# Two groups of queries and the first keys of two cross-attention stages made at the end of the stage ahead, and four stages' transfers reordered

## What is computed

```python
x = x + tanh(g_xattn[0]) * attention0(ln(x), ctx, ctx)      # 16 heads of 16
x = x + tanh(g_ffn[0])   * position_experts(ln(x))          # 8 experts, each for its 14 positions
x = x + tanh(g_xattn[1]) * attention1(ln(x), ctx, ctx)
x = x + tanh(g_ffn[1])   * lora_experts(ln(x))
x = x + tanh(g_xattn[2]) * decoder_block(ln(x), ctx)        # self-attention, cross-attention, relu layer
x = x + tanh(g_ffn[2])   * product_key_experts(ln(x))
x = x + tanh(g_xattn[3]) * attention3(ln(x), ctx, ctx, mask, padding)
x = x + tanh(g_ffn[3])   * routed_experts(ln(x))

def attention(query, key, value):
    q, k, v = heads(query @ Wq + bq), heads(key @ Wk + bk), heads(value @ Wv + bv)
    return merge(softmax(q @ k.T * scale) @ v) @ Wo + bo
```

## Time and profile before

| | us |
|---|---|
| median of 3 runs | 2893.66 (2892.99 to 2894.96) |
| the profiled execution's own time | 2895.43 |
| its span in the trace | 2893.7 |
| busy: PE, PEld | 2554.0 (88%), 2092.4 (72%) |
| busy: DVE, ACT, POOL | 1782.6 (62%), 1345.4 (46%), 1124.6 (39%) |
| the 16 DMA engines, mean share over the span | 42% |
| first cross stage begins, second, third, fourth | 313.85, 673.12, 1415.44, 2163.92 |

### The profile page before, as it was taken

One profiled execution on the slowest core, in us unless ns is written; L12 is line 12 of the kernel. 1 busy time (PEld: TensorE's weight loads), 2 busy tenths in 40 slices (PEclk: granted clock), 3 DMA queues, 4 the chain that ended last, 5 costly groups with the idle time before them and its releaser, 6 DMA issues.

```text
span 2893.7 us, 57252 instructions
## 1 busy us (share of the span) xinstructions
PE 2554.0 (88%) x21445; PEld 2092.4 (72%) x21445; DVE 1782.6 (62%) x3888; ACT 1345.4 (46%) x2700; POOL 1124.6 (39%) x1424
## 2 busy tenths in 40 slices
PE   7999789997997999869799898888868995999995
PEld 7999578794786777636477566667645884999995
DVE  5666578116784434268577445787777884566664
ACT  4444466324564121147456533444443663555563
POOL 3444411004113333247622233633543113677772
PEclk9999899997998999989789999889988996999997
DMA  8888865236660000053376300000008653565663
GB/s 229 239 244 241 220 180 166 100 120 157 164 192 16 1 1 1 19 149 87 83 190 166 125 17 6 0 1 1 1 18 212 170 136 132 195 216 205 205 222 111
DMA packets 145580, 357.06 MB, mean 123 GB/s; under 512 B 26064, under 2 KB 102480, under 8 KB 130816
## 3 DMA queue, kind: packets, MB, share of 16 engines
q1 hardware_dynamic: 133584, 268.38, 32.9%
q0 software_dynamic: 11760, 85.51, 8.3%
HBM read 260.55 MB, written 84.54 MB: 119 GB/s over the span
## 4 chain that ended last, share of the span: by engine, by line
PE 59%; DVE 11%; DMA 9%; POOL 6%; issue 6%; ACT 5%; SPq 2%; PEld 0%; POOLq 0%; PEldq 0%; ACTq 0%; DVEq 0%
PE ps L3156 8%; PE ps L1190 6%; PE ps L1200 6%; PE ps L1174 5%; DMA key_parts<-arena 5%; PE ps L3167 5%; PE ps L1745 3%; POOL arena L428 2%; PE ps L2347 2%; PE ps L2106 2%; PE ps L928 2%; PE ps L2340 2%; PE ps L2096 2%; PE ps L2056 2%; PE ps L1187 2%
## 5 line engine op out<-in xcount | busy, mean ns | idle before, releaser
L1304 ACT ACTIVATE arena<-ps 125x448 f32<-125x448 f32 x768 | 405.4, 545 | 293.0 <-PE ps L1190 289.3
L1337 DVE TENSOR_REDUCE arena<-ps 112x2 f32<-112x750 f32 x384 | 348.3, 930 | 97.8 <-PE ps L1174 96.3
L502 POOL TENSOR_SCALAR ln_var<-ln_mv 112x1 f32<-112x1 f32 x160 | 43.3, 270 | 746.7 <-DVE ln_mv L496 742.2
L1190 PEld LDWEIGHTS ps<-arena,wreg 98*125 98x125 bf16 x2304 | 217.7, 144 | 86.1 <-issue 45.3
L1190 PE MATMUL ps<-arena,wreg 98*125 98x112 bf16 x2304 | 238.8, 229 | 27.0 <-issue 17.5
L3156 PE MATMUL ps<-moe_x_r,moe_w_r 128*128 128x256 f32 x2016 | 254.4, 287 | 4.1 <-DVE arena L3312 2.7
L3156 PEld LDWEIGHTS ps<-moe_x_r,moe_w_r 128*128 128x128 f32 x2016 | 248.4, 194 | 7.3 <-DVE arena L3312 3.9
L1174 PE MATMUL ps<-wreg,arena 96*112 96x375 bf16 x768 | 203.6, 352 | 23.7 <-DMA arena<-arena 12.9
L1200 PE MATMUL ps<-arena 125*17 125x112 f32 x6144 | 201.8, 265 | 0.6 <-ACT arena L1304 0.6
L428 POOL TENSOR_TENSOR arena<-arena 128x375 bf16<-128x375 f32 x128 | 113.8, 913 | 171.2 <-ACT arena L365 171.2
L285 PE MATMUL ps<-kv_ctx_r,kv_w_r 128*128 128x376 f32 x768 | 145.9, 339 | 22.9 <-DVE kv_w_r L391 14.6
(11 more groups left out here) (367 smaller groups left out, 5860.8 us busy)
## 6 DMA issues: line engine op xcount, KB each, us to landing
wreg<-key_parts SPq DMA_DIRECT2D x288, 187.5 KB, 3.9
key_parts<-arena SPq DMA_DIRECT2D x128, 281.2 KB, 4.1
values<-arena SPq DMA_DIRECT2D x64, 357.0 KB
arena<-values SPq DMA_DIRECT2D x64, 357.0 KB
arena<-query_parts SPq DMA_DIRECT2D x84, 224.0 KB, 4.3
arena<-key_parts SPq DMA_DIRECT2D x96, 187.5 KB, 3.9
wreg<-in_e_w SPq DMA_DIRECT2D x16, 704.0 KB, 5.4
query_parts<-arena SPq DMA_DIRECT2D x14, 672.0 KB, 6.1
```

Of the source, the lines that this page charges most:

```text
L1190: mm = pe.matmul(ps[0:KN, bank, g * T:(g + 1) * T], keys[r][:, hd, c * KN:(c + 1) * KN], queries(b)[:, hd, :], start=not masked, stop=not ...
L1304: act.activation(probs[k % PROBS], ps[0:KN, 4 + k % 2, 0:GT], ACT.Exp, scale=scale).then_inc(at_probs, 1)
L1337: dve.tensor_reduce(negmax[r % 2][:, 2 * p:2 * p + 2], ps[0:T, 2 * (p % 2):2 * (p % 2) + 2, 0:S2], AX.X, ALU.max, negate=True).then_inc(at ...
```

## The change

`context_stage` and `position_experts_stage` get an object `CrossAhead` of the cross stage that follows. At their end they load keys 0 of that stage, project, split and (group 0) spread its groups 0 and 1. The cross stage then projects only groups 2 and 3: group 2 between the pairs of batch 0, group 3 behind `maxima(0, 0)` and one pair of batch 1. All four cross stages get another order on SP: values 2 and the store of group 3 move from step 0 to steps 1 and 2, and values 3 behind rows(2). In `self_stage` the gains are loaded ahead of group 1, and POOL's wait for them moves from the stage's start to its fourth batch. The diff without its places in memory:

```diff
@@ context_stage
                 step(B - 1, 1, None)
+                ahead.load_keys(sp)
@@ tensor
-                pe.wait_ge(kv_vout, B * NKV * 2)
-                for b in range(B - LAG, B):
-                    norm.turn(pe, b, turned(TURN_BANK + 2 * (b % 2)), LAG)
+                pe.wait_ge(loaded, ahead.q.ready)
+                pe.wait_ge(part_res, ahead.q.q0 - 2)
+                for g in range(AHEAD):
+                    ahead.q.project(pe, range(g, g + 1))
+                    if g == 0:
+                        pe.wait_ge(kv_vout, B * NKV * 2)
+                    norm.turn(pe, B - LAG + g, turned(TURN_BANK + 2 * g), LAG)
@@ scalar
+                ahead.q.high_and_middle(act, range(1))
                 norm.apply(act, B - 1)
+                ahead.spread(act, range(2))
+                ahead.q.high_and_middle(act, range(1, AHEAD))
+                ahead.spread(act, range(2, PARTS))
@@ vector
-                for b in range(B - LAG, B):
-                    evacuate(dve, b, turned(TURN_BANK + 2 * (b % 2)))
+                for g in range(AHEAD):
+                    ahead.q.remainders(dve, range(g, g + 1))
+                    evacuate(dve, B - LAG + g, turned(TURN_BANK + 2 * g))
@@ gpsimd
+                pool.wait_ge(ln_ready, norm.before("ready", B))
+                ahead.q.low(pool, range(AHEAD))
@@ cross_stage, sync
-                load_keys(sp, keys[0], kv, 0, 0)
+                if not ahead:
+                    load_keys(sp, keys[0], kv, 0, 0)
...
-                q.spread_first(sp, 0, group_q[0], Q_PART, group_in[0])
+                if not ahead:
+                    q.spread_first(sp, 0, group_q[0], Q_PART, group_in[0])
...
-                for g in range(1, G - 1):
+                for g in range(1, made_ahead or G - 1):
                     q.store(sp, g)
                 load_values(0, 0)
...
                 rows(0)
+                for g in range(made_ahead or G - 1, G - 1):
+                    q.store(sp, g)
...
                     if b == 0:
                         q.stored(sp, G - 2)
                         load_queries(1, range(len(Q_PART)))
+                    if b == 1:
                         load_values(2, 2)
+                        load_values(3, 3)
+                    if b == 2:
                         q.store(sp, G - 1, q_last)
-                    if has(b, 3):
+                    if b > 0 and has(b, 3):
                         at_least(sp, at_pv, (n0 + b) * STEPS if has(b, -1) else 0)
                         load_values(b + 3, place(3))
@@ tensor
-                q.project(pe, range(G - 1))
+                beside = made_ahead or G - 1
+                q.project(pe, range(made_ahead, beside))
...
-                        q.project_tile(pe, G - 1, tile, (chunk,))
-                arrived(1, 1, turn0)
-                pair(1, 1, 0)
-                maxima(0, 0)
-                pair(1, 1, 1)
+                        q.project_tile(pe, beside, tile, (chunk,))
+                if ahead:
+                    maxima(0, 0)
+                    arrived(1, 1, turn0)
+                    pair(1, 1, 0)
+                    q.project(pe, range(beside + 1, G))
+                    pair(1, 1, 1)
...
@@ vector
+                if ahead:
+                    q.remainders(dve, range(made_ahead, G - 1))
+                    reduce_pair(1, 1, 0)
                 q.remainders(dve, range(G - 1, G))
@@ self_stage
             def sync(sp):
+                norm.load(sp)
                 inputs.load(sp, 1)
-                norm.load(sp)
...
-                pool.wait_ge(loaded, loaded_all)
...
+                            if k == 3 and g * GB + b == 3:
+                                pool.wait_ge(loaded, loaded_all)
@@ position_experts_stage, sync
                 sp.wait_ge(loaded, following.ready)
+                sp.wait_ge(ffn_out, E * DC)
+                ahead.load_keys(sp)
+                ahead.spread(sp)
@@ tensor
                     if b % GB == GB - 1 and b > GB:
                         for q in range(GB):
                             norm.turn(pe, b - 2 * GB + 1 + q, slots[q % 2], 2)
+                        g = b // GB - 2
+                        if g >= 0:
+                            if g == 0:
+                                pe.wait_ge(loaded, following.ready)
+                            ahead.q.project(pe, range(g, g + 1))
@@ scalar
                         norm.evacuate(act, b - 1, slots[(b - 1) % 2])
+                    if b % GB == GB - 1 and b > GB and b < B - 1:
+                        g = b // GB - 1
+                        ahead.q.high_and_middle(act, range(g, g + 1))
@@ gpsimd
+                    if g >= G - AHEAD:
+                        pool.wait_ge(ln_ready, norm.before("ready", (g + 1) * GB))
+                        ahead.q.low(pool, range(g - G + AHEAD, g - G + AHEAD + 1))
+                        pool.wait_ge(part_lo, ahead.q.q0 + (g - G + AHEAD + 1) * DC)
@@ vector
+                    if g >= G - AHEAD:
+                        ahead.q.remainders(dve, range(g - G + AHEAD, g - G + AHEAD + 1))
```

More of the change, by code:

```diff
@@ L688, in load, with spread_first @@
                     self.weights.load(sp)
-            def spread_first(self, sp, kind, dest, order, arrived):
-                for level, made in enumerate((part_hi, part_mid, part_lo)):
+            def spread_first(self, sp, kind, dest, order, arrived, levels=range(PARTS)):
+                for level in levels:
+                    made = (part_hi, part_mid, part_lo)[level]
                     sp.wait_ge(made, self.q0 + (kind + 1) * DC)
@@ L728, in remainder, with high_and_middle @@
             def remainder(self, n):
-                return self.rest[n % len(self.rest)]
-            def high_and_middle(self, act):
+                return self.rest_ahead[n] if n < len(self.rest_ahead) else self.rest[n % len(self.rest)]
+            def high_and_middle(self, act, some=range(G)):
                 def middle(g, j):
```

108 lines of the change are left out of this document (73 added, 35 removed).

## The result

The changed kernel takes 2860.02 us (median of 4 runs, 2856.35 to 2865.80), the kernel before 2894.31 (2892.99 to 2895.72) beside it: a ratio of 0.9883, 95% interval 0.9863 to 0.9904, faster by 34.3 us. Forecast were 2859.5 and 34.3 us, with a range of 2848 to 2875. But the profiled execution of the changed kernel is its slowest, 2865.80 (span 2864.1) against 2895.43 before, so between the two traces only 29.6 us are to be found, and the runs of the changed kernel spread over 9.4 us where those of before spread over 2.7.

The account below looks back on a forecast made before the run. Bound by the way to PE's steady cross-stage steps: late queries, holes before step 2, POOL's late self-attention start. 23.3 + 0 + 0 + 11.0 = 34.3 us off 2895.43 gives 2861.1, median 1.8 lower: 2859.5; range 2848 to 2875.

Parts of the forecast that it names:

- 15.8: Starts of first and second cross stages: us from first pair to first scores, as PE waits for group 3.
- The order on SP: All four cross stages: rows(2) no longer last, holes and slow clock go; 5.3 + 8.5 + 6.0 + 3.5 = 23.3 us.
- The holes: PE idle before step 2 of the cross stages; given back 4.0 of 4.52, 4.4 of 5.79, 4.35 and 2.06 us.
- The clock's share: Slow clock behind the holes: 4.1 us in the second cross stage, 1.3, 1.7 and 1.4 in the others by hole length.
- The tail of the context stage: End of context stage: barrier 7.3 us later, first scores 1.0 earlier, nothing gained; between 6 lost and 6 gained.
- The tail of the experts' stage: End of position experts' stage: barrier at 683.0, first scores at 699.1 instead of 698.62, no gain; between 7 lost and 7 gained.
- The self-attention: Self-attention's start: POOL starts at 1267.4 instead of 1278.80; 11.0 us gained, between 8 and 11.4.
- The rival that spoke of the hole moving: Cross stages: values 2 or rows(3) become late instead; all 23.3 lost gives 2882.5, half 2871; chance 0.15.
- Tails in series: Ends of context and experts' stages: little overlaps, barriers about 11 us later than worked out, 2881; chance 0.08.
- Slower by the clock: First two cross stages: PE stays at clock 0.50 through steps, 2903 with four slow steps in each; chance 0.02.
- The clock rule: Starts of first two cross stages: pairs begin cold, each start some 2 us longer, 4 us less in the sum.
- other rule, of two rings on one set of engines: Context stage's end: sixth spreading transfer shares with keys 1, lands perhaps 1 us later; 33 instead of 34 in sum.

Follow-up runs that it names:

- SP's order alone: Kernel before with values 2 and 3 behind rows(2) and group 3's store in step 2, all cross stages: 2899.09 us, ratio 0.9945.
- context's tail: Changed kernel with next group's queries ahead of their step's values, position experts' stage and second cross stage's start as before: 2870.04 us, ratio 0.9861.
- spread by SP: Changed kernel with next group's queries ahead of their step's values and the context stage's spread issued by SP, not ACT: 2854.68 us, ratio 0.9845.

## Why the prediction was right, point by point

The total is right by luck in part: the order gave less than its 23.3 us, the experts' tail and the self-attention more than theirs, and the waits for queries took some back. Two small slips in its sums change nothing: 2861.1 less 1.8 is 2859.3, and 10.4 and 5.2 are 15.6, not 15.8.

**The order on SP, 23.3 us.** By the changed kernel's trace the four starts gave 1.8, 9.5 (to step 3), 5.9 and 5.7, 22.9 us, which looks like the forecast. It holds the experts' tail and the chance of two executions. Over the fourteen traces the four cross stages are shorter with the new order, waits for queries taken off (in the fourth not), by:

| cross stage | length taken | old order (3 traces) | new order | gain | forecast |
|---|---|---|---|---|---|
| first | C1 | 221.3 | 215.6 (3, no tail) | 5.8 | 5.3 |
| second | C2 | 358.8 | 354.0 (4, no experts' tail) | 4.8 | 8.5 |
| third | last spreading transfer to last marker | 205.7 | 203.0 (11) | 2.7 | 6.0 |
| fourth | last marker of the third to its own | 771.6 | 768.0 (11) | 3.6 | 3.5 |

The sum is 17 us, and SP's order alone measured 16 (10 to 22). Single traces of a row differ by 1 to 5.5 us. The holes went as told: no "issue" piece over 1.5 us before step 2 in any stage. The terms of the second and the third stage were too large. They rest on one trace of the kernel before, whose holes there are 5.79 and 4.35 us, while the two other kernels with the old order have 4.83 and 4.69, 3.27 and 3.87; and with the new order PE still stands 0.4 to 2.1 us wherever the chain waits for values 2 before step 2. The clock's share was not worked out by the rule given for it, either: by the lengths of the holes the 4.1 us would give 3.2, 3.1 and 1.5 for the other stages, not 1.3, 1.7 and 1.4. In the first two stages the changed kernel's own rows hide a swap, too. "Values 2 land about a microsecond after step 1 ends; in the second likewise" was too small for the order alone: without the tail steps 1 to 2 of the second stage are 13.8 to 15.5 us, 3 to 5 above a steady step. It became true by the experts' tail, which the forecast had priced at nothing.

**The tail of the context stage, 0.** Right: C1 is 215.4 us in the mean with it and 215.6 without. Its terms were less so: the barrier fell 8.6 us later, not 7.3, since ACT's issue was 0.96 us a transfer, not 0.61, within the 0 to 1.2 kept open. The last spreading transfer was taken at "some 4 us" and needs 5.26; the same transfer takes 5.36 in the kernel before. The first pair came 2.8 us earlier by the same clock of the start, not 4.2; the first scores (341.02, with the head start of 1.2) 1.1 us later, not 1.0 earlier. The profiled run lost 3.5 us to the forecast for this stage: its marker of step 2 stands 70.8 us behind the last remainder, those of the seven other traces with this tail 67.5 to 69.6, and of the three with SP's order and no tail 67.8 to 69.8. In nine of these eleven traces the chain waits for values 2 just before step 2; in the changed kernel's and in "context's tail" it does not, since step 1 itself comes late there, behind keys 2.

**The tail of the experts' stage, 0.** This is the step that failed. "The transfers have landed by then, so the first pair is at 683.3 instead of 687.38, and with the same 15.8 us the first scores at 699.1: no gain": on the scale of the kernel before (4.0 us added) the barrier fell at about 681, the first pair at 681.3 and the first scores at 698.9. That looks right, but only beside a trace whose own first scores are the earliest of seven; by the table above the first scores came 3 us earlier, and step 2 another 4. The prediction said that SP's work there lies beside an idle queue and did not ask what that work, out of the way, does for the next late transfer. The tail was worth some 6 us, near the end of the 7 kept open.

**The self-attention, 11.0.** 12.8 over the fourteen traces, 13.0 in the changed kernel's, 11.6 (7.3 to 16) alone. POOL's start moved by 11.3, as told; in the cross stages the prediction had counted the slow clock behind a stall and here left it out.

**The changes of groups: no term.** The forecast took the steady steps as untouched because nothing in the diff touches them. Their length is, but one step in four waits for a load, and that wait was longer in this trace: the second stage lost 3.6 us behind its step 3 and the third 2.3 behind its step 2, nearly all of it at changes of groups. The steady steps are as before (10.74). By Q the loss is 5.6 us in the pair of traces and 4.7 in the means (13.0 against 8.3), which just about cancels the experts' tail.

**The rival that spoke of the hole moving** (0.15) was half right in mechanism for the first two stages; the order gave some 17 us of the 23.3, where this rival left half or nothing. Tails in series: the experts' barrier came 8 us later, not some 21. Slower by the clock: no stretch of slow steps came.

**The clock rule.** Between the first pair and the first scores of the first stage the changed kernel needs 16.4 us and in the second 17.6, where I had 15.8. The trace shows the clock lower there: windows of the first start, changed kernel and kernel before (the first begins 4 us earlier; over 322 to 341 us the changed kernel has 0.77):

```profile
318.00:341.00 23.00, 13.34 (x37) 6.69 (x38) 13.04 (x21) 5.61 (x11) 11.25 (x7) 0.72 0.62 160
```

```profile
322.00:341.00 19.00, 12.44 (x39) 5.83 (x37) 12.80 (x19) 6.45 (x12) 13.58 (x10) 0.91 0.82 218
```

The Trainium skill (TensorE: Matmul & The Clock Gate, "Part 1: The HAM clock gate") has the low clock as the default; by that rule the starts were to begin cold and be some 2 us longer each. The rows agree in direction: from first pair to first scores the granted clock is 0.81 against 0.87 before in the first stage and 0.76 against 1.00 in the second, and the two stretches are 0.6 and 1.8 us beyond the 15.8; no run parts the clock's share from the rest. The Trainium skill's other rule, of two rings on one set of engines (DMA: Bandwidth & Descriptors, "Queues, rings and completion order"), was to cost the sixth transfer 1 us. The trace does not show it for that transfer: it lands in 5.26 us. The six together do land later, 7.0 us in the median against 5.7 for six on SP in "spread by SP" at the same place, so the rule is not refuted. Before, the piece in front of the pair at 328.52 was:

```profile
323.13 5.36 DMA arena<-arena
```

## What to carry to other kernels

A hole in front of a step goes to the next late transfer; price that one with the bytes of the whole queue in front of it, and look for a stage ahead whose queue is idle. When a term of a sum is "nothing, no first result earlier", ask for the second and third as well. When the total comes out right, measure each term over several traces: one trace of before that happens to be early or late in a stretch makes a term look right. And a loop that is bound by compute in three steps of four can wait for a load in the fourth: read the worst step, not the steady one, and put what is needed soonest first in its queue.

## What the runs showed of the hardware

- What an issue costs its engine varies: SP's took 0.63 us each at the start of the first cross stage (six in 3.77 us from 313.88, kernel before), 0.90 each in the earlier trace rows, 0.71 each for keys 0 at the end of the context stage and 0.73 for the spread in "spread by SP"; ACT's took 0.96 each there. What sets the difference is open.
- Chips differ by more than an edit is worth: the same kernel took 2894, 2898, 2908 and 2916 us with the result and in the three sets, while its own runs in one agree within 3 us (4 runs) to 21 us (18 runs), the one of 7723 us left out. Most of it is in the stage that is bound by transfers: the context stage's end came at 302 to 305 us in two of them and at 314 to 320 in the other two.
- Unchanged stretches move, too: from the last marker of the fourth cross stage to the end the fourteen traces have 482 to 492 us. Below the 6 us of a ratio's interval only a length inside the trace, over several traces, tells two kernels apart.
